# Second attention of an audio tower: another order of the four engines' work within a batch, and the middle parts of q and k rounded on Pool

## The reference

```python
def _L1_attn_ref(sequence, ln_gamma, ln_beta, Wq, bq, Wk, bk, Wv, bv, Wo, bo, mu):
    mean = jnp.mean(sequence, axis=-1, keepdims=True)
    var = jnp.mean(jnp.square(sequence - mean), axis=-1, keepdims=True)
    x = (sequence - mean) / jnp.sqrt(var + EPS) * ln_gamma + ln_beta
    q = _split_heads(x @ Wq.T + bq)
    k = _split_heads(x @ Wk.T + bk)
    v = _split_heads(x @ Wv.T + bv)
    scores = jnp.einsum('bhqd,bhkd->bhqk', q, k) / scale
    scores = jax.nn.sigmoid(scores - mu) * jnp.exp(scores)
    scores = scores / jnp.sum(scores, axis=-1, keepdims=True)
    out = jnp.einsum('bhqk,bhkd->bhqd', scores, v)
    ...
    return out @ Wo.T + bo
```

## Time and profile before

| | us |
|---|---|
| median of 3 runs | 779.65 |
| lowest, highest | 774.19, 780.9 |
| span of the profiled execution | 779.1 |

### The profile page before, as it was taken

How to read it: one execution, slowest core, us unless ns; L and a number is a source line. 1 busy time by engine, 2 the same in 40 slices (tenths; PEclk the granted TensorE clock), 3 DMA queues, 4 the chain that set the end, 5 groups by cost and what they waited for, 6 DMA issues and landing times.

```text
span 779.1 us, 16167 instructions
## 1 busy us (share of the span) xinstructions
PE 707.4 (91%) x5688; PEld 580.0 (74%) x5696; DVE 442.6 (57%) x1125; ACT 357.8 (46%) x610; POOL 129.2 (17%) x166
## 2 busy tenths in 40 slices
PE   5687999999989999999999999998899999998635
PEld 4466878878768999999999999996566665665423
DVE  3557688888673342344222232332788898866666
ACT  3242454345533212122212112213998989988435
POOL 2010122232132210000001001002634222210000
PEclk9699999999999999999999999999999999999855
DMA  6979166355737566555555555571875447651002
GB/s 172 213 133 262 31 97 102 79 86 87 121 109 268 189 209 223 189 192 172 180 189 181 199 192 177 169 180 46 101 113 95 67 63 104 82 65 18 1 14 95
DMA packets 70839, 102.54 MB, mean 132 GB/s; under 512 B 8416, under 2 KB 58600, under 8 KB 70640
## 3 DMA queue, kind: packets, MB, share of 16 engines
q1 hardware_dynamic: 67376, 93.15, 50.7%
q0 software_dynamic: 3136, 8.40, 4.2%
q10 hardware_dynamic: 256, 0.07, 0.0%
HBM read 63.75 MB, written 12.58 MB: 98 GB/s over the span
## 4 chain that ended last, share of the span: by engine, by line
PE 61%; DVE 17%; ACT 7%; DMA 7%; issue 5%; POOL 1%; SPq 1%; ACTq 1%; DVEq 0%; POOLq 0%
PE psum L1981 18%; PE psum L2032 17%; DVE arena L1304 9%; DMA arena<-arena 5%; PE psum L1661 4%; PE psum L1924 3%; PE psum L1685 2%; PE psum L1930 2%; ACT arena L830 2%; PE psum L1939 1%; POOL w0T L699 1%; PE psum L2009 1%; DVE arena L1157 1%; PE psum L2149 1%; PE psum L1654 1%
## 5 line engine op out<-in xcount | busy, mean ns | idle before, releaser
L1981 PEld LDWEIGHTS psum<-arena 128*128 128x128 f32 x1248 | 144.9, 192 | 2.1 <-issue 0.3
L1981 PE MATMUL psum<-arena 128*128 128x128 f32 x1248 | 146.1, 275 | 0.1
L2032 PE MATMUL psum<-arena 128*128 x624 | 141.4, 380 | 0.8 <-DVE arena L1450 0.8
L859 ACT ACTIVATE arena<-psum,arena 128x128 f32<-128x128 f32 x156 | 44.5, 368 | 194.7 <-PE psum L1981 115.2
L2032 PEld LDWEIGHTS psum<-arena 128*128 128x128 f32 x624 | 115.5, 190 | 15.4 <-issue 1.2
L1432 DVE TENSOR_SCALAR arena<-psum,arena 128x128 f32<-128x128 f32 x156 | 44.0, 345 | 80.5 <-PE psum L1981 67.3
L1939 PE MATMUL psum<-arena 96*128 96x256 bf16 x512 | 75.1, 274 | 9.1 <-ACT arena L829 5.7
L1304 DVE TENSOR_TENSOR arena<-arena 128x1024 f32<-128x1024 f32 x64 | 79.9, 1316 | 4.5 <-ACT arena L829 2.6
L1939 PEld LDWEIGHTS psum<-arena 96*128 96x128 bf16 x512 | 44.3, 97 | 44.0 <-ACT arena L829 14.4
L699 POOL DMA_INDIRECT w0T<-yg,pos x32 | 37.4, 1169 | 222.6 <-DMA yg<-arena 176.2
L1450 DVE TENSOR_TENSOR arena<-psum,arena 128x256 f32<-128x256 f32 x39 | 16.6, 425 | 96.6 <-PE psum L2032 96.6
(11 more groups left out here) (290 smaller groups left out, 1207.8 us busy)
## 6 DMA issues: line engine op xcount, KB each, us to landing
arena<-in_L_ffn_w_dram SPq DMA_DIRECT2D x47, 1024.0 KB, 5.1
arena<-arena SPq DMA_DIRECT2D x192, 128.0 KB, 5.1
arena<-xg SPq DMA_DIRECT2D x39, 128.0 KB, 2.0
yg<-arena SPq DMA_DIRECT2D x39, 128.0 KB, 1.7
out_dram<-arena SPq DMA_DIRECT2D x8, 256.0 KB, 2.1
xg<-zeros SPq DMA_DIRECT2D x9, 128.0 KB, 2.9
arena<-in_x_dram SPq DMA_DIRECT2D x8, 128.0 KB, 3.1
arena<-in_L_ffn_b_dram SPq DMA_DIRECT2D x1, 1024.0 KB, 14.9
```

What stands on the lines that cost most here:

```text
L859: ins = act.activation(hidT[:, v, c, :], psum[:, 2 * v, c * P:(c + 1) * P], ACT.Relu, bias=b1c[:, v, c:c + 1])
L1981: mm = pe.matmul(psum[:, 2 * v + c // HALF, (c % HALF) * P:(c % HALF + 1) * P], w1b[:, i % W1_BUFS, d, c * P:(c + 1) * P], xtT[:, v, d, :] ...
L2032: mm = pe.matmul(y_bank, hidT[:, u, c, :], w2s[:, one(e), c, :].rearrange("p o n -> p (o n)"), start=(c == 0), stop=(c == HC - 1))
```

## The change

- **Pool**: copies the middle parts of q and k of batch b+1 (was ScalarE's `second_part`). Its iteration b opens with gather(b+2) (was gather(b+3), behind combine(b+2) of VectorE's iteration b), then bias of h for batch b (was b-1), `scale1` of b-2 for the second norm, `scale1` of b+2 for the first, and the two copies.
- **ScalarE**: the two `turned_x` stand together after the second function, the copy of the values behind the third instead of the second, both `second_part` are gone.
- **VectorE**: `combine` and `stat1` are for batch b+3 and stand behind the multiplies; the maximum is of batch b-2 and stands between rest and last part of q; q's rest and last part come before k's; the sum with h comes after all of them; the second norm closes the iteration.
- **PE**: `turned_input` behind the first score pair, the values of groups 2 and 3 one pair later, the output projection one pair later, `values` behind the first pair of pass 2, values' group 0 before the seventh pair; six idle products instead of ten.

SP's queue is unchanged. The new helpers that are left out here hold the bodies of the lines they replace, with the batch counted as their own b. A line of "..." leaves out moved bodies.

```diff
--- before.py
+++ after.py
@@ -701,20 +701,32 @@
                                 in_offset=bass.IndirectOffsetOnAxis(ap=pos[:, c, b * QT + q:b * QT + q + 1], axis=0)
                             ).then_inc(y_in[b % 2], 16)
+                def biased_h(b):
+
+                    pool.wait_ge(S["n_xh"], QT * (b + 1))
+                    v = h[:, bass.ds(b * QT, QT), :]
+                    pool.tensor_tensor(v, v, bo1[:].rearrange("p (o d) -> p o d", o=1).to_broadcast([P, QT, D]),
+                                       ALU.add).then_inc(S["n_hbo"], 1)
+
+                def second_part(b, which, got, done):
+
+                    pool.wait_ge(got, b + 1)
+                    pool.tensor_copy(n_qkp[which][:, 1], n_qkr[which]).then_inc(done, 1)
+
                 def iteration(b, u, k):
-                    if stages(b - 1, 0, LAST):
-                        pool.wait_ge(S["n_xh"], QT * b)
-                        v = h[:, bass.ds((b - 1) * QT, QT), :]
-                        pool.tensor_tensor(v, v, bo1[:].rearrange("p (o d) -> p o d", o=1).to_broadcast([P, QT, D]),
-                                           ALU.add).then_inc(S["n_hbo"], 1)
-                    if stages(b + 3, 4, LAST):
-                        gather(b + 3)
-                    if stages(b + 2, 0, LAST):
+                    if stages(b + 2, 3, LAST):
+                        gather(b + 2)
+                    if stages(b, 0, LAST):
+                        biased_h(b)
+                    if stages(b - 2, 0, LAST):
+                        scale1(b - 2, 1, S["m_mv"], S["m_eps"], S["m_rstd"])
+                    if stages(b + 2, 3, LAST):
                         scale1(b + 2, 0, S["n_mv"], S["n_eps"], S["n_rstd"])
+                    if stages(b + 1, 1, LAST):
+                        second_part(b + 1, 0, S["n_qr"], S["n_qm"])
+                        second_part(b + 1, 1, S["n_kr"], S["n_km"])
                     if b == 0:
-                        gather(3)
-                    if stages(b - 1, 0, LAST):
-                        scale1(b - 1, 1, S["m_mv"], S["m_eps"], S["m_rstd"])
+                        scale1(2, 0, S["n_mv"], S["n_eps"], S["n_rstd"])
                 for b in range(2):
...
@@ -899,17 +923,21 @@
                                 act.wait_ge(S["y_ev"], MOE_TILES)
                             function(first[:, u, p], area[p % 2], FIRST[u]).then_inc(S["f1_done"], 1)
+                    def pass2(p):
+                        if stages(b, 0, LAST):
+                            act.wait_ge(S["s2_mm"], PAIRS * b + p + 1)
+                            products_made(act, b, p - 4)
+                            function(second[:, p % 4], area[p % 2], FIRST[v]).then_inc(S["f2_done"], 1)
+
+                    pass1(0)
+                    pass1(1)
                     if stages(b + 1, 1, LAST):
                         turned_x(b + 1, 0)
-                    pass1(0)
                     if stages(b + 1, 1, LAST):
                         turned_x(b + 1, 1)
-                    pass1(1)
+                    pass1(2)
                     if stages(b - 1, 0, LAST):
-                        act.wait_ge(S["n_pv"], 4 * b)
-                        wait(act, S["n_ot1"], b - 1)
-                        act.copy(n_oa, pv_out).then_inc(S["n_oa"], 1)
-                    pass1(2)
+                        copied_oa(b - 1)
                     pass1(3)
                     if stages(b + 1, 0, LAST):
                         high(b + 1, 0, S["n_q_mm"], S["n_stkq"], S["n_qh"])
@@ -917,21 +945,18 @@
                     if stages(b + 1, 0, LAST):
                         high(b + 1, 1, S["n_k_mm"], S["n_stkk"], S["n_kh"])
                     if stages(b - 1, 0, LAST):
-                        act.wait_ge(S["n_ot2"], b)
-                        wait(act, S["n_wo"], b - 1)
-                        act.copy(n_oT.rearrange("p c t -> p (c t)"), misc[0]).then_inc(S["n_oT"], 1)
-                    if stages(b + 1, 0, LAST):
-                        second_part(b + 1, 0, S["n_qr"], S["n_qm"])
+                        copied_oT(b - 1)
                     pass1(5)
-                    if stages(b + 1, 0, LAST):
-                        second_part(b + 1, 1, S["n_kr"], S["n_km"])
                     pass1(6)
                     pass1(7)
-                    if stages(b, 0, LAST):
-                        for p in range(PAIRS):
-                            act.wait_ge(S["s2_mm"], PAIRS * b + p + 1)
-                            products_made(act, b, p - 4)
-                            function(second[:, p % 4], area[p % 2], FIRST[v]).then_inc(S["f2_done"], 1)
+                    pass2(0)
+                    pass2(1)
+                    pass2(2)
+                    pass2(3)
+                    pass2(4)
+                    pass2(5)
+                    pass2(6)
+                    pass2(7)
                 all_batches(iteration)
...
@@ -1499,49 +1524,83 @@
...
                 def iteration(b, u, k):
                     v = 1 - u
-                    if stages(b + 2, 3, LAST):
-                        combine(b + 2)
                     if stages(b - 1, 0, LAST):
...
+                        turned_sums(b - 1)
+                    if stages(b - 1, 0, LAST):
+                        divided(b - 1)
                     if stages(b + 1, 0, LAST):
                         wait(dve, S["n_qm"], b + 1)
                         split_rest(b + 1, 0, S["n_qh"], S["n_qr"])
+                    if stages(b - 2, 0, LAST):
+                        maximum(b - 2)
+                    if stages(b + 1, 0, LAST):
+                        split_last(b + 1, 0, S["n_qm"], S["n_ql"])
+                    if stages(b + 1, 0, LAST):
+                        wait(dve, S["n_km"], b + 1)
                         split_rest(b + 1, 1, S["n_kh"], S["n_kr"])
-                    if b == 0:
-                        split_last(1, 0, S["n_qm"], S["n_ql"])
-                        split_last(1, 1, S["n_km"], S["n_kl"])
-                        combine(2)
-                    if stages(b + 2, 2, LAST):
-                        stat1(b + 2)
-                    if stages(b + 1, 2, LAST):
-                        split_last(b + 1, 0, S["n_qm"], S["n_ql"])
-                    if stages(b - 1, 0, LAST):
...
                     if stages(b + 2, 3, LAST):
                         norm1(b + 2)
-                    if stages(b + 1, 2, LAST):
+                    if stages(b + 1, 0, LAST):
                         split_last(b + 1, 1, S["n_km"], S["n_kl"])
                     if stages(b - 1, 0, LAST):
...
+                        sum_h3(b - 1)
+                    if stages(b - 1, 0, LAST):
+                        stat2(b - 1)
+                    if b == 0:
+                        combine(2)
+                        stat1(2)
                     if stages(b + 1, 1, LAST):
                         biased_v(b + 1, v)
                     for p in range(PAIRS):
@@ -1549,20 +1608,12 @@
                             multiply(b, u, p)
                         if b == 0 and p == 2:
                             norm1(2)
+                    if stages(b + 3, 3, LAST):
+                        combine(b + 3)
+                    if stages(b + 3, 3, LAST):
+                        stat1(b + 3)
                     if stages(b - 1, 0, LAST):
...
+                        norm2(b - 1)
...
@@ -2072,26 +2131,36 @@
                                 pe.wait_ge(S["f1_done"], PAIRS * b + p - 1)
                             scores(b, u, p, S["s1_mm"])
+                    def pass2(p):
+                        if stages(b, 0, LAST):
+                            if p < 2:
+                                pe.wait_ge(S["f1_done"], PAIRS * b + 7 + p)
+                            else:
+                                pe.wait_ge(S["f2_done"], PAIRS * b + p - 1)
+                            scores(b, u, p, S["s2_mm"])
+
+                    def idle_products(n):
+                        if stages(b, 0, LAST):
+                            wait(pe, S["n_on"], QT * b)
+                            for _ in range(n):
+                                idle_product()
+
+                    pass1(0)
                     if stages(b + 1, 0, LAST):
                         turned_input(b + 1)
-                    pass1(0)
+                    pass1(1)
                     if stages(b - 1, 0, LAST):
                         weigh_values(b - 1, v, 2)
-                    pass1(1)
                     pass1(2)
+                    pass1(3)
                     if stages(b - 1, 0, LAST):
                         weigh_values(b - 1, v, 3)
-                    pass1(3)
                     if stages(b + 1, 0, LAST):
                         pe.wait_ge(S["n_xT_done"], DC * (b + 2))
                         wait(pe, S["n_h3"], b - 1)
                         project_rows(misc[0], 0, S["n_q_mm"])
                     if stages(b - 1, 0, LAST):
-                        pe.wait_ge(S["n_oa"], b)
-                        for q in range(QT):
```

(32 more changed lines are left out.)

83 lines of the change are left out of this document (52 added, 31 removed).

## The result

The changed kernel takes 773.04 us in the median of 14 runs (768.66 to 776.25), the kernel before 779.89 over the runs beside it. The ratio is 0.9919, with a 95% interval of 0.9892 to 0.9945: 0.8% faster, inside the 1% that I called "same", 1 us from the forecast of 772. The profiled execution has a span of 771.5 us against 779.1.

A forecast was written before the change was run, and what follows sets the result against it. Before, VectorE and ScalarE hand over to each other; after, VectorE's 23.8 us per batch bounds above ScalarE's 22.0. From 779.1, -3.1, -2.6, -1.1 and -0.4 total -7.2: 771.9, forecast 772; 8 in 10: 766 to 780.

The forecast's parts named there:

- ScalarE's bound: ScalarE per batch: copy of the values at M (batch's first multiply)+10.7, then 11.07; sum 21.8, taken as 22.0 us.
- VectorE's bound: VectorE per batch: fourth gather landed M+11.85, then 3.4 to the reciprocals and 8.6 to the next M; 23.8 us.
- Rival C: Pool's casts are slow, 2.17 us each, held by VectorE's two-input work; 2.5 us a batch, total 785; chance 0.11.
- I read this as the multiplies keeping Pool out: Batch 0's 6.00 us gather, ending 0.9 after five back-to-back multiplies, was taken to show that VectorE's multiplies block Pool's gathers.
- The term of +0.95 behind the last multiply: In steady batches the fourth gather starves under the multiplies and ends at M + 9.1 + 0.95, landing at M + 11.85.
- B: Rival: no gather starves; Pool's sum still holds the multiplies 1.1 us, stretches 22.8, total 768; chance 0.20.
- E: Rival: stacks of q and k land late for pass 1's first score; about +1 each, inside the other cases, no own chance.
- Batch 0: no gain: Combine(3) waits for the same gather as before, so M(1) stays at the old 577.0.
- rival D: With 4 idle products fewer PE may get the lower clock; +3 us a batch, 790 if in all; chance 0.07.
- A score function ahead of the copy: On ScalarE, a third pass-1 function before the copy of the values fills idle time and takes 0.95 from the 13.05 us part.
- the casts: Two 128x512 copies per batch leave ScalarE for Pool, taking 2 x 0.52 = 1.03 us off ScalarE's 13.05 us part.
- costed at nothing: On PE, 4 of 10 idle products go, about a microsecond that nobody waited for; no cost unless the clock needs it.

The follow-up runs named there:

- spreads_held: Changed kernel, SP sending the middle and last parts of batch 1's stacks only after batch 0's last multiply; 784.29 us in its one run.
- gap_later: Changed kernel with the normalisation of batch 2 behind the fifth instead of the third multiply of batch 0; 772.78 us in its one run.
- both_moves: Changed kernel, combine(2) and its statistics heading VectorE's iteration 0; from batch 4 Pool's bo1 sum and scale of b-2 precede the gathers; 778.37 us.
- gathers_early: Changed kernel, Pool doing bo1 sum and scale of b-2, then gather of b+3, then scale of b+2 and casts; batch 0 keeps its order; 776.68 us.
- ten_idle: Changed kernel with ten idle products in PE's pass 2 as before instead of six; 768.68 us, ratio 0.9883.
- The first two experiments: Kernel before with only the casts moved to Pool, 777.96 us; the same with the output projection's halves one score pair later, 778.93 us.
- casts_back: Changed kernel with the two casts of q and k back on ScalarE at their old places; 783.11 us, ratio 1.0045.

## Why the prediction was right, and where it was not

**ScalarE's bound: right, 0.2 to 0.5 short.** The copy of the values was put at M+10.7 and came at M+10.80 in batch 1. The part behind it was put at 11.07 + 0.2 and took 11.55 to 11.80 (11.65 in batch 5, where no gather takes part): the wait of 0.47 for the score behind the transposition of the values (637.97) is new, and the sum had 0.2 for it. Batch 1 to 2 was 22.35 for 22.0, batch 5 to 6 22.50 for 22.0, batch 6 to 7 21.23 for 21.0.

**VectorE's bound: right.** Reciprocals to M take 8.78 in batches 1 and 3 (590.02 to 598.80, and 637.53 to 646.31) and up to 9.04 in the others, for 8.6. Pool's cast is 0.61, and 0.73 beside VectorE, where I took 0.9; 0.61 is below the range's 0.64. Rival C is out. But VectorE waits for PE before the reciprocals, 0.77 to 1.54 in batches 1 to 4 and 3.81 in batch 5: it isn't the bound.

**"I read this as the multiplies keeping Pool out": the step that failed.** In batch 0 it fits: for 2 of the gather's 5.67 us nothing but multiplies ran (spreads_held), and another place of the break let it through (gap_later). Carrying it to the steady batches was wrong: the fourth gather waited for the next multiply to end and no longer, as all four do in both_moves. The term of +0.95 behind the last multiply and the wait before combine (2 to 3 us) didn't occur. The trace of the kernel before had a row against it, a gather that began under the first of three back-to-back multiplies (552.04, 553.19, 554.32) and got in at the next one:

```profile
552.75 1.42 POOL L699 DMA_INDIRECT w0T<-yg,pos  x1 [0.19 <-issue]
```

The Trainium skill, "SBUF — State Buffer", section "Who interferes with whom", infers that a tensor_tensor with both inputs in SBUF leaves descriptor generation alone. In this case it did not hold for the gathers that began under a multiply, 1.3 to 2.0 us instead of 0.95 where more than 0.2 us of it were left, and least for the one of 5.67.

**Why the total still fits.** Two rivals that I had kept apart came together. B's hold of the multiplies by Pool's sum was priced at 1.1 and is 1.09, in batches 2 to 4. E, the late stacks, was priced as "about +1, inside the other cases"; I had put it in no sum. In batches 3 and 4 it is about 0.65 on top. 22.35 + 1.1 is 23.45 for batch 2, and 22.35 + 1.1 + 0.65 is 24.1 for batches 3 and 4, beside the 23.8 of a mechanism that wasn't there. The kernel without expert rows shows that both hang on the gathers, and not on the shorter batch from which I had reasoned to E. The rest is luck: ahead of M(0) the profile has 3.75 us that the forecast lacks, 1.6 of them from work that the change doesn't touch, and 3.1 of them go again in batch 0. Where gathers are placed moves their price but doesn't take it away: 1.5 a batch beside the stacks, 2.62 of wait when they go under the multiplies, 2.20 of wait and a slowed last part ahead of the casts.

**"Batch 0: no gain" was wrong twice.** Ahead of M(0) 2.15 us were gained (13.0 from the first gather of batch 2 to M(0) instead of 15.1). The kernels with Pool's casts and the new order have 13.0 to 13.5 there but for the two with the early combine, those with one of the two alone 15.0 to 16.0, so it takes both. Behind M(0) 3.1 were lost by the wait for the projection at the lower clock. That is rival D's mechanism with another place and price: I looked for it in the steady batches, where the clock is 1.00 throughout, and it struck once, after 2.51 us of idle PE that follow from VectorE's wait for the late gather. As gathers_early and ten_idle idle as long and keep the clock, whether it strikes is not forecast by the idle time alone.

**"A score function ahead of the copy" and the casts**: 0.95 + 1.03 were added up as if each stood alone. The first two experiments and casts_back show that they are one change: moving the casts is worth nothing with the old order, and the new order costs 0.45% without it, a part of that by the clock.

**Idle products "costed at nothing"**: not refuted. Six were enough for the full clock in every steady batch of the changed kernel and over the gap in gathers_early; whether ten do better on the whole is open, as told above.

What stays open too is why the one gather in batch 0 let the starts of four multiplies pass, in nine kernels, with 5.67 us in eight of them and 6.00 in the kernel before, while those in the steady batches and in both_moves got in at the first. In the changed kernel the gather began at 553.25 and the multiplies behind it at 553.48, 554.62, 555.75 and 556.89; it ended 0.8 after the record of the last. Moving a single VectorE instruction (gap_later) ended this.

## What to carry to other kernels

Before the time of an engine's removed work is counted, look at what that work covered on the engine that feeds it: here 1.03 us of casts hid 1.01 us of waits for scores. A transfer that is moved into a better place for its engine should be priced at every queue that it then shares, and two rivals that hang on the same cause should be priced together. A single long duration in a trace shows that a thing can happen, not that it will in each batch; the neighbouring rows that did not show it are part of the evidence.

## What the runs showed of the hardware

An indirect gather of 128 rows on Pool takes 0.95 us with 0.30 to the next, 1.3 to 2.0 under back-to-back multiplies of VectorE with two SBUF inputs, and in one place 5.67, without any transfer, PE or ScalarE work beside it for 2 us of that. Pool rounds 128x512 from f32 to bf16 in 0.61 us, 0.73 beside VectorE. The granted clock after 2.5 us of idle PE was 0.50 over 4 us in the changed kernel and 1.00 in gathers_early, with the same PE work ahead of the gap: 6.91 and 6.90 us busy of the first 8 from M(0), 3.93 and 3.93 of the next 4, 3.98 and 3.99 of the last 4.
